# A graph network over one 4096 x 4096 adjacency in eight passes: three split steps of pass 3 kept on chip for pass 4, and W1 applied behind the first multiplication

## The reference

```python
x = ln(x + A @ (f2 * (A @ (relu(A @ (f1 * (A @ (x @ W1)))) @ W2))))
x = ln(x + concat(x, A @ x) @ weight)
m = x @ W_msg + b_msg                              # gated layer
g = sigmoid((m @ W_q) @ (m @ W_k).T / sqrt(128) + gate_bias) * A * A
x = ln(x + ln_affine(relu(concat(x, g @ m) @ W_upd + b_upd)))
h = silu(A @ x @ W3 + b3)
x = ln(x + silu(A @ h @ W3 + b3))
```

## Time and profile before

| | |
|---|---|
| runs | 1667.01 us median of 3 (1663.84 to 1667.1) |
| the profiled execution | 1666.21 us, its span 1664.4 us |
| PE busy | 1609.0 us (97%), granted clock 0.993 of full |
| DVE busy | 1212.8 us (73%) |
| ACT busy | 1099.7 us (66%) |
| DMA | 484.56 MB, mean 291 GB/s |

### The profile page before, as it was taken

How to read it: one execution, slowest core, us unless ns; L and a number is a source line. 1 busy time by engine, 2 the same in 40 slices (tenths; PEclk the granted TensorE clock), 3 DMA queues, 4 the chain that set the end, 5 groups by cost and what they waited for, 6 DMA issues and landing times. The chain is left out here.

```text
span 1664.4 us, 19276 instructions
## 1 busy us (share of the span) xinstructions
PE 1609.0 (97%) x7674; PEld 767.7 (46%) x7674; DVE 1212.8 (73%) x1181; ACT 1099.7 (66%) x784; POOL 54.2 (3%) x49
## 2 busy tenths in 40 slices
PE   7999999999999998999999899999999999999997
PEld 4444444444444444444554444444353444444443
DVE  6866538654766478556899598998989986554886
ACT  5667747764878567755667487796878786454743
POOL 2000000000000000000000000100000100000001
PEclk9999999999999999999999999999999999999999
DMA  9979798979799888996878354554545898764972
GB/s 368 414 301 381 284 419 345 371 284 415 286 388 426 340 317 346 382 340 270 321 283 315 129 202 177 177 207 172 201 166 190 322 371 304 268 250 162 363 276 109
DMA packets 67562, 484.56 MB, mean 291 GB/s; under 512 B 7712, under 2 KB 7872, under 8 KB 9232
## 3 DMA queue, kind: packets, MB, share of 16 engines
q1 hardware_dynamic: 66240, 478.70, 74.6%
q0 software_dynamic: 1088, 4.56, 0.8%
q10 hardware_dynamic: 144, 0.07, 0.0%
HBM read 414.09 MB, written 69.21 MB: 290 GB/s over the span
## 5 line engine op out<-in xcount | busy, mean ns | idle before, releaser
L989 DVE SCALAR_TENSOR_TENSOR a_lo<-a_ring,a_hi 128x2048 f16<-128x2048 f32 x320 | 723.9, 2288 | 301.1 <-ACT a_hi L792 296.9
L792 ACT ACTIVATE a_hi<-a_ring 128x2048 f16<-128x2048 f32 x320 | 604.9, 1905 | 279.4 <-PE spare L594 153.2
L594 PE MATMUL acc<-a_hi,y_hi 128*128 128x512 f16 x1536 | 460.5, 381 | 5.5 <-ACT a_hi L792 3.5
L594 PE MATMUL acc<-a_hi,y_lo 128*128 128x512 f16 x1536 | 460.4, 381 | 0.0
L606 PE MATMUL acc<-a_lo,y_hi 128*128 128x512 f16 x1536 | 406.0, 379 | 7.9 <-DVE a_lo L998 4.9
L606 PEld LDWEIGHTS acc<-a_lo,y_hi 128*128 128x128 f16 x1536 | 149.7, 98 | 192.6 <-DVE a_lo L998 8.1
L594 PEld LDWEIGHTS acc<-a_hi,y_lo 128*128 128x128 f16 x1536 | 150.8, 98 | 182.8 <-issue 2.9
L594 PEld LDWEIGHTS acc<-a_hi,y_hi 128*128 128x128 f16 x1536 | 150.5, 98 | 183.2 <-issue 8.1
L1011 DVE SCALAR_TENSOR_TENSOR gates<-gates,a_ring 128x1024 f32<-128x1024 f32 x128 | 156.1, 1220 | 35.1 <-ACT gates L822 34.8
L805 ACT ACTIVATE a_hi<-gates 128x1024 f16<-128x1024 f32 x128 | 134.8, 1053 | 41.1 <-DVE gates L1011 40.9
L998 DVE TENSOR_TENSOR a_lo<-gates,a_hi 128x1024 f16<-128x1024 f32 x128 | 155.8, 1217 | 0.0
(11 more groups left out here) (119 smaller groups left out, 763.6 us busy)
## 6 DMA issues: line engine op xcount, KB each, us to landing
a_ring<-adj_dram SPq DMA_DIRECT2D x326, 1024.0 KB, 7.4
saved_squares<-squares SPq DMA_DIRECT2D x64, 1024.0 KB, 12.7
a_ring<-saved_squares SPq DMA_DIRECT2D x64, 1024.0 KB, 4.8
x_T<-xt_dram SPq DMA_DIRECT2D x4, 512.0 KB, 8.1
x_rows<-x_dram POOLq DMA_DIRECT2D x1, 2048.0 KB, 12.8
out_dram<-x_rows POOLq DMA_DIRECT2D x3, 512.0 KB, 3.0
out_dram<-x_rows SPq DMA_DIRECT2D x2, 256.0 KB, 2.0
w<-W_dram POOLq DMA_DIRECT2D x2, 64.0 KB, 5.2
```

Of the source, the lines that this page charges most:

```text
L594: mm = pe.matmul(sums[:, h * BANK:(h + 1) * BANK], blk(y[:, y_pass % 2, :], st.j0 + s), slot(a_hi, st)[:, s, h * BANK:(h + 1) * BANK], sta ...
L792: act.activation(slot(a_hi, st), loaded(st), ACT.Copy, scale=2.0 ** A_EXP).then_inc(s_ahi, 1)
L989: dve.scalar_tensor_tensor(out=slot(a_lo, st).rearrange("p s c -> p (s c)"), in0=loaded(st).rearrange("p s c -> p (s c)"), scalar=2.0 ** A ...
```

## The change

- `KEPT` becomes a table by pass. Beside the six steps of pass 7, three steps of pass 3 (block (1, 1), t = 1, 2, 3) get their halves in `x_T` (two of them) and in `xn` and `tmp`, outside the ring of four; pass 4 uses them with no load and no split. Pass 7's four kept steps in `squares` lie there in another arrangement.
- Since block (1, 1) is no longer loaded whole in pass 4, its squares are made in pass 3; those of block (2, 2) move from pass 3 to pass 4.
- `lead` takes the later of two places for a step only where a second use of a kept step lies between.
- Pass 0 has no projection: SP loads x itself, chunk by chunk, into `x_rows` between the first steps, and ACT and DVE split it into y directly. `project` of pass 1 multiplies `z_T` by W1 in place of the transposes. POOL's load of x goes.

```diff
-            (3, 2): 3, (1, 2): 4, (0, 1): 4, (3, 3): 3, (2, 2): 3, (1, 1): 4, (0, 0): 4}
+            (3, 2): 3, (1, 2): 4, (0, 1): 4, (3, 3): 3, (2, 2): 4, (1, 1): 3, (0, 0): 4}
...
-KEPT = [(i, (j * GROUP + t) * SJ) for i, j, t in ((0, 0, 1), (0, 0, 2), (0, 2, 2), (0, 2, 3), (1, 3, 0), (1, 3, 1))]
+IN_SQUARES, IN_X_T, IN_ROWS = RING, RING + SQUARE_SLOTS, RING + SQUARE_SLOTS + 2
+KEPT = {3: dict(zip(kept_steps((1, 1, 1), (1, 1, 2), (1, 1, 3)), (IN_X_T + 1, IN_ROWS, IN_X_T))),
+        7: dict(zip(kept_steps((0, 0, 1), (0, 0, 2), (0, 2, 2), (0, 2, 3), (1, 3, 0), (1, 3, 1)),
+                    (IN_SQUARES, IN_SQUARES + 1, IN_SQUARES + 2, IN_SQUARES + 3, IN_X_T, IN_X_T + 1)))}
...
-                if p == PASSES and at in KEPT:
+                if at in KEPT.get(p - 1, ()):
                     group.append(kept[at])
                     continue
...
-            return max(n, FIRST_USE[st.n] - RING) if st.p == PASSES else n
+            return max(n, FIRST_USE[st.n] - RING) if any(n <= u < FIRST_USE[st.n] for u in SECOND_USES) else n
...
             for ic in range(NC):
-                sp.dma_start(x_T[:, ic * CH:(ic + 1) * CH], xt[:, ic * CH:(ic + 1) * CH]).then_inc(s_xt[ic], 16)
+                sp.dma_start(x_chunk(0, ic), x[:, ic * CB:(ic + 1) * CB, :]).then_inc(s_x[ic], 16)
                 load(STREAM[ic])
...
-                elif p == 0:
-                    by_node((x_T_chunk(p, k), w1[:, :]))
+                elif p == 1:
+                    by_node((z_T, w1[:, :]))
...
             stages = {
-                0: {0: [project]},
                 1: {2: [project, query_key_weights]},
...
-                if p in (0, 2, 5):
+                if p == 0:
+                    act.wait_ge(s_x[k], 16)
+                elif p in (2, 5):
                     act.wait_ge(s_rows, nth("rows", p, k, PER_CHUNK["rows"][p] - 1))
...
-            pool.wait_ge(s_alo, STEPS * NC)
-            pool.dma_start(x_rows[:, :, :], x).then_inc(s_x, 16)
```

More of the change, by code:

```diff
@@ L65 @@
 PER_CHUNK = {
-    "rows": {0: 1, 1: 1, 2: 1, 3: 1, 4: 2, 5: 5, 6: 1, 7: 1, 8: 1},
+    "rows": {1: 1, 2: 1, 3: 1, 4: 2, 5: 5, 6: 1, 7: 1, 8: 1},
     "x_T": {4: 1, 5: 1},
@@ L118, with kept_steps @@
 Unit = namedtuple("Unit", "step p k use s first last")
-KEPT = [(i, (j * GROUP + t) * SJ) for i, j, t in ((0, 0, 1), (0, 0, 2), (0, 2, 2), (0, 2, 3), (1, 3, 0), (1, 3, 1))]
+def kept_steps(*steps):
+    return [(i, (j * GROUP + t) * SJ) for i, j, t in steps]
+IN_SQUARES, IN_X_T, IN_ROWS = RING, RING + SQUARE_SLOTS, RING + SQUARE_SLOTS + 2
+KEPT = {3: dict(zip(kept_steps((1, 1, 1), (1, 1, 2), (1, 1, 3)), (IN_X_T + 1, IN_ROWS, IN_X_T))),
+        7: dict(zip(kept_steps((0, 0, 1), (0, 0, 2), (0, 2, 2), (0, 2, 3), (1, 3, 0), (1, 3, 1)),
+                    (IN_SQUARES, IN_SQUARES + 1, IN_SQUARES + 2, IN_SQUARES + 3, IN_X_T, IN_X_T + 1)))}
 def plan():
@@ L135, in plan @@
                 steps.append(group[-1])
-                if p == PASSES - 1 and at in KEPT:
+                if at in KEPT.get(p, ()):
                     kept[at] = group[-1]
@@ L163 @@
 for _st in STREAM:
-    _keep = _st.p == PASSES - 1 and (_st.i, _st.j0) in KEPT
-    SLOT.append(RING + KEPT.index((_st.i, _st.j0)) if _keep else sum(s < RING for s in SLOT) % RING)
-    HALVES_BEFORE.append(_holds.get(SLOT[-1]))
+    _kept = KEPT.get(_st.p, {})
+    SLOT.append(_kept.get((_st.i, _st.j0), sum(s < RING for s in SLOT) % RING))
+    HALVES_BEFORE.append(_holds.get(SLOT[-1]) if SLOT[-1] < RING else None)
     _holds[SLOT[-1]] = _st.n
@@ L171 @@
 SQUARED_BEFORE = [sum(n < m for n in SQUARED) for m in range(len(STREAM) + 1)]
+SECOND_USES = [n for n, u in enumerate(UNITS) if u.p != u.step.p]
 SAVED = sorted((p, k) for p, k, use in SUM_DONE if use == "next")
@@ L263, in build @@
         s_small = sem("small_loaded")
-        s_w1, s_x = sem("w1_loaded"), sem("x_loaded")
-        s_xt = [sem(f"xt_loaded{i}") for i in range(NC)]
+        s_w1 = sem("w1_loaded")
+        s_x = [sem(f"x_loaded{i}") for i in range(NC)]
         s_a = [sem(f"a_loaded{i}") for i in range(LOADS)]
@@ L350, in halves_free @@
                 eng.wait_ge(used, freed(st))
-            elif n >= RING + SQUARE_SLOTS:
+            elif n >= IN_ROWS:
+                eng.wait_ge(s_wqk_product, 1)
+                eng.wait_ge(s_bias, 2 * BIAS_STEPS)
+            elif n >= IN_X_T and st.p > GATED:
                 eng.wait_ge(s_rows, nth("rows", GATED, NC - 1))
-            elif n >= RING:
+            elif IN_SQUARES <= n < IN_X_T and st.p > GATED:
                 eng.wait_ge(s_lg, NB * NC)
+            elif IN_SQUARES <= n < IN_X_T:
+                for t in range(SQUARE_SLOTS):
+                    eng.wait_ge(s_stored[t], 16 * len(SQUARED) // SQUARE_SLOTS)
         def loaded(st):
@@ L363, in slot @@
                 return t[:, n, :, :]
-            if n < RING + SQUARE_SLOTS:
-                v = squares[:, n - RING, :].bitcast(F16)
-            else:
-                v = x_T[:, (n - RING - SQUARE_SLOTS) * SJ * CH:(n - RING - SQUARE_SLOTS + 1) * SJ * CH].bitcast(F16)
-            at = 0 if t is a_hi else SJ * CH
+            if n < IN_X_T:
+                c = n - IN_SQUARES
+                pair = squares[:, 0:SJ, :] if t is a_hi else squares[:, SJ:2 * SJ, :]
+                return pair.bitcast(F16)[:, :, c * CH:(c + 1) * CH]
+            if n == IN_ROWS:
+                v, at = (xn_T if t is a_hi else tmp_T).bitcast(F16), 0
+            else:
+                v = x_T[:, (n - IN_X_T) * SJ * CH:(n - IN_X_T + 1) * SJ * CH].bitcast(F16)
+                at = 0 if t is a_hi else SJ * CH
             return v[:, at:at + SJ * CH].rearrange("p (s c) -> p s c", s=SJ)
@@ L526, in project @@
                 if p == 1 and k == 0:
+                    pe.wait_ge(s_w1, 16)
+                if p == 3 and k == 0:
                     pe.wait_ge(s_id, 1)
                     pe.wait_ge(s_small, SMALL)
-                if p in (1, 3, 4):
+                if p in (3, 4):
                     transposes(lambda b: blk(z_T, b))
@@ L891, in split_biases @@
                     dve.wait_ge(s_small, SMALL)
-                    dve.wait_ge(s_rows, nth("rows", 0, NC - 1))
+                    dve.wait_ge(s_rows, nth("rows", 1, NC - 1))
                     dve.memset(bupd_rows, 0.0).then_inc(s_zeroed, 1)
@@ L988, in split_low @@
                 halves_free(dve, st, s_unit)
[L989 to L992, removed]
+                dve.scalar_tensor_tensor(out=slot(a_lo, st), in0=loaded(st), scalar=2.0 ** A_EXP, in1=slot(a_hi, st),
+                                         op0=ALU.mult, op1=ALU.subtract).then_inc(s_alo, 1)
             def gate_low(u):
```

11 lines of the change are left out of this document (2 added, 9 removed).

## The result

The changed kernel took **1677.38 us** (median of 4 runs, 1675.41 to 1678.28), the kernel before 1667.05 in the same comparison. The ratio is 1.0069, with a 95% interval of 1.0047 to 1.0091. I had said 1670.0, with a range of 1661.0 to 1674.5: the direction of the likeliest case was right, its size was not, 10.3 us in place of 3.4, and the range did not reach it. The profiled execution, the slowest of the four (1678.28 us), has a span of 1676.4 us, 12.0 more than before.

A forecast was written before the change was run, and what follows sets the result against it. PE was taken to bound passes 1 and 2, with waits at the start and in later passes. Terms -6.0 + 3.6 + 3.9 + 1.7 + 0.2 = +3.4 on 1666.21 gave 1669.6, stated as 1670.0, range 1661 to 1674.5.

The forecast's parts named there:

- The start: Beginning of the kernel: without the four projections, step 19 ends at 69.9 in place of 75.95, a gain of 6.0 us.
- the gain is lost at the first close: Rival, chance 0.12: a wait of 2 us at the first close and low clock leave 2.3 of the start's 6.0; 1673.7 us.
- W1 behind pass 1: Projection behind pass 1: products with W1 take 0.91 us more than transposes for each of four chunks; costs 3.6 us.
- Pass 3: Pass 3's first transposes: moved squares and their writes make z_T 3.9 us later, and a low clock costs 1.7 more.
- the first rival: Rival, chance 0.20: ACT alone binds, not the loads, so z_T of pass 3 is ready at 456.4, 2.4 us later.
- The low clock: After PE's longer wait in pass 3, a stretch of 3.41 us at clock 0.50 costs 1.7 us.
- Pass 4: Moved squares make PE 5.5 us late at the beginning, kept steps give 5.3 back; net +0.2, bounds -5.3 and +2.
- The gain at chunk 1: Pass 4: kept steps remove the wait of 3.60 us before chunk 1's transposes and its low clock's 1.7; 5.3 back.
- Writes yield to loads: Rival, chance 0.20: in passes 3 and 4 loads get through beside the writes and ACT alone binds; -1.0, 1665.6 us.
- The squares cost nothing: Rival, chance 0.18: ACT and loads run ahead enough in passes 3 and 4; -7.7, 1659.0 us.
- That kept steps don't help: Rival, chance 0.03: in pass 4 z_T of chunk 1 stays late and the 5.3 don't come back; +8.7, 1675.3 us.
- That loads run at no more than 358 GB/s: Rival, chance 0.02: HBM limits loads, a step's load outlasts its products, the start gains nothing; +9.4, 1676.0 us.

The follow-up runs named there:

- start_only: The changed kernel with pass 3's kept steps and the exchange of the two squared blocks undone, only the new start left: 1663.29 us, ratio 0.9987 to the kernel before.
- kept_only: The changed kernel with the start as it was before; pass 3's kept steps and the exchange of squared blocks stay: 1679.44 us, ratio 1.0078 to the kernel before.
- no_writes: The changed kernel with the eight squares of blocks (1, 1) and (2, 2) made on ACT but not written to HBM: 1664.74 us, ratio 0.9985.
- no_squares: The changed kernel with blocks (1, 1) and (2, 2) neither squared nor written: 1658.86 us, ratio 0.9961.
- squared_in_2: The changed kernel with block (1, 1) squared in pass 2 and (2, 2) in pass 3: 1660.67 us, ratio 0.9964; measured again 1658.03 us, ratio 0.9949.
- none_kept: The changed kernel with block (1, 1) squared in pass 2, (2, 2) in pass 3, and without pass 3's kept steps: 1663.98 us, ratio 0.998 to the kernel before.
- filled: The changed kernel with 38 and 32 additional unread PE products before the first transposes of passes 3 and 4: 1674.09 us, ratio 1.0055 to the kernel before.

## Why the prediction was wrong

**The start, -6.0: right in size, in part by luck.** 6.2 in the changed kernel, 6.9 in start_only. I had left the landing of load 19 at 64.8 and let step 19 wait for it. It was issued at 55.6 and landed 8.1 later, at 63.7, and step 19 did not wait: PE's last wait before it, 0.43 us for a low half, is at 48.14. The loads bound earlier than I had it, between 26 and 48 us. That the gain is lost at the first close (0.12) did not happen.

**W1 behind pass 1, +3.6: right**, but for "nothing else is added". With squares due in pass 2, `z_T` of its first chunk is now 0.74 late on ACT (0.60 in start_only).

**Pass 3, +3.9 and +1.7: the mechanism right, the wait mis-sized.** This is the step that failed: "load 110 lands at 434.0; then write, load 111, write, ... at 2.47 each". The price of a pair held, 4.9 us. What failed is the first link, "a load with nothing ahead lands 4.8 after its issue", for a load that has a write ahead and one right behind. The 4.8 of the earlier trace rows is the median of pass 6's loads of saved squares, with no write beside them. By 427.3, when load 110 was issued, the write of square 104 was still under way, and that of 105 came 0.4 behind; it took 8.8, 4.0 more than I gave it. With everything 1.9 early, my 434.0 becomes 432.1, and `z_T`'s 457.8 becomes 455.9. Load 110 landed at 427.3 + 8.8 = 436.1, and `z_T`, begun at 459.34 with 1.22 to go, was ready at 460.56: 4.7 late. Load 113 in between was to land at 446.9 and landed at 451.6, 4.7 late as well, so what was added after it had the right size. My 3.9 and these 4.7 make 8.6, and the low clock 1.5: the 10.0. That the start was early has no part in it, since kept_only waits 8.59 without it. ACT alone I had sized rightly: the first rival's 456.4, 1.9 earlier, is 454.5, and in no_writes the transposes begin at 454.72.

**The low clock, +1.7: right in size for pass 3** (1.5). I had looked for one stretch of 3.41 us; it was 10.24, but 7.1 of it lay in PE's idle time. In pass 4 I had 1.7 as well, and it was 2.9.

**Pass 4, +0.2: wrong by 3.3, and outside its bounds (+2).** The gain at chunk 1, 5.3, was exact. The loss at the beginning was 8.8, not 5.5: a wait of 7.1 (I had 5.0) and 2.9 of low clock (I had 1.7), less the old 1.20 which hides in it. The wait is the loads again: load 149, with nothing ahead and a write 0.4 us behind, took 6.4 and not 4.8, and load 154 landed at 633.3, where mine, 8.1 later by then, stood at 631.0.

**The sum:** -6.2 + 3.6 + 0.7 + 10.0 + 3.5 = 11.6, against 12.0 between the spans.

**The rivals.** "Writes yield to loads" (0.20) fell: they did the opposite, and taking the writes away was worth 14 us. Its sum, 1665.6, is about what no_writes gives, ratio 0.9985. "The squares cost nothing" (0.18) fell too: at these two places they and their writes cost what no_writes and no_squares gave back. Its time is reached only where the squares are left out (0.9961) or stand elsewhere (squared_in_2). That kept steps don't help (0.03) is refuted by none_kept. That loads run at no more than 358 GB/s (0.02) is refuted again: 428 GB/s of loads and writes in the stretch of the first wait, and the start's 6.2 us, which that rule would not have left. My bounds for pass 3 were 0 and 6.5, and both doubtful sizes, the loads' landing and the clock, were bounded by the same few rows in which writes and loads were already in step; there is the fault of the range.

## What to carry to other kernels

Work that is moved takes its place in queues along: a square of 1.9 us on ACT was the small part, its 1 MB of write beside the loads that the next close waits for was the large one. Look where a stretch has halves in hand on ACT, on DVE and bytes free on the DMA engines, all three, and put such work there; the same squares in the middle of pass 2 cost nothing that could be seen. And when a transfer's landing is estimated in a stretch with others, count those that were issued before it and are still under way, and those issued right behind it.

## What the runs showed that I had not expected

- A load of 1 MB from HBM took 4.9 us alone, and 8.8 with one write of 1 MB ahead still under way and one issued 0.4 us behind: what is issued later takes its share from what is under way. The Trainium skill ("DMA: Bandwidth & Descriptors", section "Queues, rings and completion order") says that the descriptors of a queue are taken up in order, while a later one may finish before an earlier one, so that completion does not follow the order of issue. The trace shows the overlap, since a load with one write behind it took 6.5 us; a later transfer landing first it does not show, as the loads and writes from 421.4 to 435.8 landed in the order of their issue (427.9, 430.4, 436.1, 438.5, 441.8, 444.3, 446.6, 449.1). Between the landings of loads 109 and 110 the DMA engines were nearly always busy (0.94) and yet moved 325 GB/s, where the next stretch has 423. Why, these runs don't show. By stretch, the changed kernel:

```profile
427.90:436.10 8.20, 8.20 (x40) 3.72 (x38) 4.58 (x2) 8.20 (x6) 0.00 (x0) 1.00 0.94 325
436.10:441.80 5.70, 5.70 (x29) 2.55 (x27) 5.11 (x3) 4.18 (x4) 0.00 (x0) 1.00 1.01 423
```

- The low clock lasted 10.24 us behind waits of 8.60 and 7.14, and 3.4 behind 3.60 and 1.95. Behind 1.49 it did not come. In filled, products whose results nobody reads kept it away.
